# Layer 1 attention: GpSimd makes both LayerNorm roots ahead of the adding transfers of a step

## The reference

```
x = x + tanh(g_xattn[0]) * L0_xattn(layernorm(x), ctx)
x = x + tanh(g_ffn[0])   * L0_ffn(layernorm(x))        # 8 experts, top 2, plus a shared one
x = x + tanh(g_xattn[1]) * L1_xattn(layernorm(x), ctx, mask)
x = x + tanh(g_ffn[1])   * L1_ffn(layernorm(x))        # 32 experts, top 4, plus a shared one

layernorm(x) = (x - mean(x)) / sqrt(var(x) + 1e-5)
L1_xattn: 16 heads, 77 context tokens; softmax(Q K^T / 8, masked) V, then W_O
L1_ffn:   logits = h @ gate_w.T; top 4 of softmax, renormalised;
          each token's row goes to its experts' slots; the results are added back to its row
```

## Time and profile before

| | |
|---|---|
| median of the timed runs | 1073.92 us |
| span of the profiled execution (first to last instruction) | 1089.7 us |
| PE busy | 916.8 us (84%) |
| DVE busy | 653.2 us (60%) |
| ACT busy | 478.0 us (44%) |
| POOL busy | 552.4 us (51%) |
| mean granted TensorE clock | 0.900 |
| adding transfers `x_res<-y_d` | 14 of 512 KB, median 11.7 us to landing |
| POOL's DMA queue (q0) | 33792 packets, 46.46 MB |
| SP's DMA queue (q1) | 112882 packets, 121.87 MB |

### The profile page before, as it was taken

The page is one execution under the profiler, slowest core; times in us unless marked ns, Lnnn a source line. Parts: engine busy times, 40 slices in busy tenths (PEclk is TensorE's granted clock), DMA queues, the critical chain, the costliest instruction groups (busy, mean ns, idle before and its releaser), DMA issues. The chain is left out here.

```text
span 1089.7 us, 18645 instructions
## 1 busy us (share of the span) xinstructions
PE 916.8 (84%) x5465; PEld 771.4 (71%) x5465; DVE 653.2 (60%) x2191; ACT 478.0 (44%) x1753; POOL 552.4 (51%) x624
## 2 busy tenths in 40 slices
PE   4998769999999698888648999999999979999920
PEld 3663447888787487787538889999999966888710
DVE  4603035767676456565437799999999963444431
ACT  1313552322332145544337677778877731222100
POOL 1400123455555535555534766666666653777861
PEclk8879988889898799999868899999999979999975
DMA  9522885668786966767499963623413005999689
GB/s 306 185 93 62 234 231 140 164 201 232 224 229 183 240 210 206 213 216 239 131 272 196 221 164 103 231 76 138 126 53 99 16 11 151 261 248 240 70 192 158
DMA packets 163957, 189.71 MB, mean 174 GB/s; under 512 B 16035, under 2 KB 145209, under 8 KB 163858
## 3 DMA queue, kind: packets, MB, share of 16 engines
q1 hardware_dynamic: 112882, 121.87, 38.4%
q0 software_dynamic: 33792, 46.46, 19.7%
q10 hardware_dynamic: 17184, 20.19, 5.4%
HBM read 96.19 MB, written 103.63 MB: 183 GB/s over the span
## 5 line engine op out<-in xcount | busy, mean ns | idle before, releaser
L1747 POOL DMA_INDIRECT slots_d<-rows,place x128 | 131.2, 1025 | 71.4 <-DVE place L1967 40.1
L1806 ACT ACTIVATE att<-bank,mx 128x77 f32<-128x77 f32 x512 | 160.6, 357 | 0.7 <-DVE mx L1883 0.5
L1806 ACT ACTIVATION_READ_ACCUMULATOR att<-bank,mx 128x1 f32 x512 | 122.0, 238 | 0.0
L960 POOL DMA_INDIRECT y_d<-rows,targets x78 | 79.5, 1019 | 72.8 <-DVE rows L1291 49.9
L2065 PE MATMUL bank<-vwo_hi,attT_hi 128*128 128x256 f32 x320 | 96.0, 300 | 1.3 <-DVE attT_lo L1898 1.3
L2066 PE MATMUL bank<-vwo_lo,attT_hi 128*128 128x256 f32 x320 | 92.8, 290 | 0.0
L2067 PE MATMUL bank<-vwo_hi,attT_lo 128*128 128x256 f32 x320 | 92.6, 289 | 0.0
L2065 PE MATMUL bank<-wqk_hi,xa_hi 128*128 128x462 f32 (+1 forms) x192 | 76.7, 399 | 6.3 <-DVE xa_lo L1888 5.0
L1313 PE MATMUL bank<-wd_hi,act_hi 128*128 128x256 f32 (+1 forms) x206 | 71.3, 346 | 1.6 <-POOL act_lo L921 0.9
L927 POOL DMA_INDIRECT slots_d<-rows,place x64 | 63.8, 996 | 15.9 <-issue 15.6
L2067 PE MATMUL bank<-wqk_hi,xa_lo 128*128 128x462 f32 (+1 forms) x192 | 68.2, 355 | 0.0
(11 more groups left out here) (303 smaller groups left out, 2724.3 us busy)
## 6 DMA issues: line engine op xcount, KB each, us to landing
expert_gate_up<-in_wgu SPq DMA_DIRECT2D x40, 256.0 KB
rows<-slots_d SPq DMA_DIRECT2D x39, 260.0 KB
slots_d<-zrow SPq DMA_DIRECT2D x8, 1168.0 KB
expert_rows<-slots_d SPq DMA_DIRECT2D x32, 292.0 KB
x_res<-y_d POOLq DMA_DIRECT2D x14, 512.0 KB, 11.7
expert_down<-in_wd SPq DMA_DIRECT2D x40, 128.0 KB
wqk_d<-wqk SPq DMA_DIRECT2D x32, 154.0 KB, 3.6
vwo_d<-vwo SPq DMA_DIRECT2D x16, 308.0 KB
```

Of the source, the lines that this page charges most:

```text
L960: pool.indirect_dma_start(y0_d, bass.IndirectOffsetOnAxis(ap=tgt0[:, s % NY0, b:b + 1], axis=0), y_rows(s, b), None, bounds_check=T * K0 - ...
L1747: pool.indirect_dma_start(slots_d, bass.IndirectOffsetOnAxis(ap=place[:, n % 3, k:k + 1], axis=0), rows[:, n % 3, :], None, bounds_check=S ...
L1806: last = act.activation(att[:, par, h * S:(h + 1) * S], bank[:, a, i * S:(i + 1) * S], ACT.Exp, scale=-1.0, bias=mx[:, par, h:h + 1], accu ...
```

## The change

In each step POOL now makes the root of LayerNorm a for the next tile and the root of LayerNorm b first, and issues the step's adding transfers after them. Before, it issued the adding transfers first. The dispatch stays last. Nothing is added or removed.

```diff
                     def step(n, par, scores, values, routes, dispatch):
+                        if scores and n + 1 < TILES:
+                            rstd("a", n + 1, 1 - par)
+                        if routes:
+                            rstd("b", n - 2, par)
                         if n < CHUNKS - 1:
                             add_experts(*((n // 2 * 2 + 1, n % 2) if n < CHUNKS - 2 else (CHUNKS - 1, 0)))
                             if n < CHUNKS - 2:
                                 add_experts(n // 2 * 2 + 2, n % 2)
                         if n == CHUNKS - 1:
                             add_experts(CHUNKS - 1, 1)
-                        if scores and n + 1 < TILES:
-                            rstd("a", n + 1, 1 - par)
-                        if routes:
-                            rstd("b", n - 2, par)
                         if dispatch:
```

## The result

The changed kernel takes 1071.99 us in the median of 20 runs, the kernel before 1076.86 us in the median of 20 runs taken beside them (one run of the changed kernel, of 3014.6 us, and one of an experiment, of 1183.06 us, were disturbed and count in no comparison). The ratio is 0.9952, 95% interval 0.9935 to 0.9969: faster by 5 us of 1077. The 20 runs of the kernel before include the three shown above, but their median is 3 us higher, so the forecast of 7.5 us has to be held against the ratio, not against 1066.4. A gain of 7.5 us would be a ratio of 0.9930, just outside the interval. The direction was right, the size was not, and the parts of it were wrong on both sides.

The account below looks back on a forecast made before the run. Bound by the chain of waits into DVE: tile 3's load ahead of step 2, and 6.45 us above plain in steps 2 to 7, mostly step 4. Gains 4.5 + 3.0 = 7.5 us: 1073.9 to 1066.4 us, range 1063.5 to 1072.5.

Parts of the forecast that it names:

- the forecast of 7.5 us: Whole kernel: 4.5 us from the later steps plus 3.0 from step 1, giving 1066.4 us; chance 0.52.
- Steps 4 to 8, a gain of 4.5 us: Attention: roots no longer wait behind transfer issues; time above plain steps falls from 6.45 to 1.91 us.
- I take 0.65 for step 4: Step 4: root b comes 0.6 us late instead of 2.58, with no fall of PE's clock; 0.65 above plain.
- I take 0.45 each: Steps 5 and 6: POOL's idle time hides 2.28 of the pair's 2.84 us; 0.45 us above plain each.
- The third rival: Steps 3 and 5: POOL waits up to 4.2 and 3.9 us for landings; slower, up to 1077.5 us; chance 0.08.
- The upper bound, 8.1 us above plain steps: Steps 4 to 6 each 1.9 us late and one clock fall of 2.17: a loss of 1.7 us.
- Step 1, a gain of 3.0 us: Step 1: (1,1) issued later lets SP load tile 3's row sooner, so step 2 starts 3.0 us sooner.
- The upper bound of 4.3: Step 1: most it could gain, with DVE at tile 3's addition by 572.1 instead of going on at 576.38.
- The range for the time: Whole kernel: measured time expected between 1063.5 and 1072.5 us.
- (1,1) behind `shift_a`: Sign in step 1: POOL issues (1,1) after that root instruction, at about 567.9 instead of 565.26.
- tile 3's addition sooner: Sign on DVE: the addition of tile 3 at about 573.4 instead of 576.38.
- The sign for being wrong in the whole: Attention: line 1940 of tile 7 less than 3 us sooner than 656.84, or that gain not kept to the end.

Follow-up runs that it names:

- the second half: Against the kernel before: transfers first in steps 0 and 1 as before, roots first only from step 2 on; ratio 0.9997.
- the halves: Two kernels against the kernel before: roots first only in steps 0 and 1, ratio 0.9950; roots first only from step 2 on, ratio 0.9997.
- The experiment with step 1 alone: Against the kernel before: roots ahead of the transfers in step 1 only, everything else as before; ratio 0.9976.
- spread kernel: Against the kernel before: roots first, and from step 3 on one single transfer every other step; ratios 0.9884 and 0.9889.

## Why the prediction was wrong

**Steps 4 to 8, a gain of 4.5 us: there was none.** This is the term that failed. In the mean of two profiles of each kernel the steps 2 to 10 are 96.54 - 93.73 = 2.8 us longer; by the time of the second half (0.9997) they are between 3.3 us shorter and 2.6 us longer. Three steps of the working failed.

- "I take 0.65 for step 4": 1.45 measured. The gap between pair and dispatch was counted as 0.1 and is 0.31, and the dispatch was taken from a plain step; dispatch and root a took 586.03 - 579.03 = 7.0 us, not 6.52. This is no accident of step 4. In the seven profiles of the changed kernel and the layouts made from it (the halves aside), 41 of the 44 dispatches right behind a transfer took 5.25 to 5.76 us, while those without one took 4.88 to 4.93; one of the four instructions is then stretched (ahead of step 4 to 1.46 us instead of 0.97). The cause is open.
- "I take 0.45 each, since a part of the lateness is carried over and not paid again": it is paid again. With a pair in each step POOL has no idle time left. From root b to root b it takes 586.41 - 575.54 = 10.87 and then 597.53 - 586.41 = 11.12 us, more than a plain step's 9.67, and the step is as long as that row. The steps 5 and 6 were 1.29 and 1.67 us too long. With the pairs two steps apart each of four pairs costs 1.3 us.
- The third rival looked for landing waits in the steps 3 and 5. They came in step 5 (0.90 and 1.84 us) and in step 7, where (7,1) waited 4.43 us for the single (7,0); I had taken (7,0) and (7,1) for free since each fits in POOL's idle time. That was a price by length only; the wait of k = 1 for k = 0 can be larger. It does not come with the change alone: the kernel before had 1.55 us of it in one of its two profiles. The fall of the clock did go from step 4, as forecast, but came back in step 8 or in step 6 behind such a wait.

The upper bound, 8.1 us above plain steps, was the better figure: 10.65 and 8.36 were measured through step 10.

**Step 1, a gain of 3.0 us: right in mechanism, and not the whole.** 6.6 us were measured for the steps 0 and 1. It was right that tile 3's load was the last wait and that POOL's queue beside SP's was its reason. The missing term is step 0's pair. I wrote of step 1 only, and of (1,1); but the change also puts (1,0) and (2,0) behind a root that waits for tile 1's load, and so 5.6 us later. The experiment with step 1 alone gives 27.39 us, about 4.5 less than before, from a single long execution; its ratio is worth 2.6 us. With step 0 added it is 25.4. The upper bound of 4.3 was too low too. DVE's readiness in it was nearly right (20.5 us behind the first `veps_a` forecast, 20.1 measured), but it rests on one profile of before, whose wait for the load was 1.72 us; in the second profile it was 4.77.

**The sum** came out near by two errors of opposite sign, which is luck: 7.5 forecast; 6.6 - 2.8 = 3.8 by the profiles through step 10, 4.8 from the first `veps_a` to the last line 1940 (338.6 against 333.8 in the means); 5 by the ratio. The range for the time held it.

Of the signs that I had named, these came: (1,1) behind `shift_a`, tile 3's addition sooner (20.1 us behind the first `veps_a`, 21.8 named, 24.8 before), a clock of 1.00 through step 4, and, for rival three, a wait in step 5. These did not: step 4 of 10.3 us with a wait for root b under 1 us (1.39), steps 5 and 6 of 10.1, steps 7 and 8 of 9.7. The sign for being wrong in the whole was a line 1940 of tile 7 less than 3 us sooner. Counted from the first `veps_a` it comes 105.28 - 103.26 = 2.0 us sooner in the two first profiles, so this sign came; in the mean of two profiles each it is 4.0 us.

## What to carry to other kernels

When an issue of DMAs is moved past work of its engine, write down all its instances, the first ones included, and ask of each what else the DMA engines carry at its new time. A transfer that must wait for the landing of its twin needs a distance measured against the landing times in the trace (here 5.6 to 14.7 us for 512 KB), not against the issue's length; work that the critical engine waits for stands behind it in the same row. And where a burst of transfers is too long for the idle time of a step, deal it out in pieces that fit: the piece of 1.44 us cost at most 0.2 us, the pair of 2.7 us cost 1.3. Count the whole row when you ask what fits: the gap behind the issue and the longer dispatch took 1.0 us on top of the pair's length.

## What the runs showed of the hardware

Landing times of the adding 512 KB transfers, spread kernel, from the view of line 1701:

```profile
DMA to landing us min/median/max: 6.2/9.1/12.0
```

I had expected that they would fall far below a step's 9.7 us once the heavy loads of steps 0 and 1 were over. In the kernel with singles one step apart they run from 5.6 to 13.1 us, with a median of 9.4; the longest of all profiles is 14.7. That SP's own issue instruction for the 80 KB rest of `vwo_lo` in the steps 0 and 1 takes 2.94 to 3.06 us or 6.9 to 8.7 us, as POOL's queue is empty or busy, was new to me: here SP's row is a gauge for the crowding of the DMA engines.
